# A new table of places: the steps of three overlapping batches merged into one order per engine

## The chip, the core and the metric

The kernel runs on one core of a Trainium2 chip. A core has five engines that each work through their own instructions in order: PE (TensorE, the matrix unit; its weight loads are listed apart as PEld), DVE (VectorE), ACT (ScalarE), POOL (GpSimd) and SP (SyncE, which here only starts transfers). They meet through semaphores. The metric is the device time of one execution in microseconds (us); lower is better.

## The reference

Two decoder layers over `x` of 32 batches, 128 tokens and 128 features, six sublayers in all, each with a residual and a layer norm:

```python
x = _layernorm(x + _L0_attn_ref(x, w_qkv, w_proj))                 # Nystrom attention, 16 heads, 64 landmarks
x = _layernorm(x + _L0_xattn_ref(x, ctx_1024, ...))                # cross attention, 16 heads of 8, relative bias
x = _layernorm(x + _L0_ffn_ref(x, Wr, br, W1, b1, W2, b2))         # 8 experts, the best one per token
x = _layernorm(x + _L1_attn_ref(x, Wq, Wk, Wv, Wo, bo))            # causal attention, 16 heads of 8
x = _layernorm(x + _L1_xattn_ref(x, ctx, ctx, mask, ...))          # masked cross attention, 16 heads of 64
x = _layernorm(x + _L1_ffn_ref(x, fc1_A, fc1_B, ...))              # h = gelu(x @ W1); h @ W2
# inside the Nystrom attention, per head, six times:
KV = K @ V;  V = 0.25 * V @ (13 * I - KV @ (15 * I - KV @ (7 * I - KV)))
```

All numbers are float32. The batches do not depend on one another.

## The kernel before, in words

A prologue loads all weights and composes the two matrices of the last feed-forward. Then the 32 batches run, each in two parts. The first part, `nystrom`, is the first sublayer; it has one set of buffers (stream 2) and one batch is in it at a time. The second part, `rest`, is the other five sublayers; it has two sets of buffers (lanes 0 and 1), and even and odd batches alternate. So three batches are in work at once: one in `nystrom`, two in `rest` at different depths.

Each engine's program is written as Python generators, one for `nystrom` and one for `rest`, which yield a name after each step. A step is a small group of instructions with the waits ahead of it. Names that begin with `n.` belong to `nystrom`; `r1.` is the first cross attention, `rm.` the experts, `r2.` the causal attention, `ry.` the masked cross attention, `rf.` the last feed-forward, and `r.ln1` to `r.ln4` the layer norms between them. The same name on two engines is the part of a stage that each engine does. The names that the prediction uses:

- On PE, `n.proj` is the projection of a new batch, `n.a0` to `n.a3` and `n.b0`, `n.b1` the score products, `n.e3T0`, `n.e3T1`, `n.e1T0`, `n.e1T1` transposes of exponentials, `n.col0`, `n.col1` column sums, `n.kk0`, `n.kk1` and `n.y0` the start values of the iteration, `n.ln` the transpose of the finished first layer norm. `n.Skg` and `n.Wkg` are the two products of round k (0 to 5) of the iteration for half g of the heads. Between `n.Skg` and `n.Wkg` ACT copies PSUM out (L984) and DVE makes two passes (L1265, L1267); between `n.Wkg` and the next `n.S` ACT scales (L990) and DVE adds (L1275).
- On PE, `rm.h0` to `rm.h3` and `rm.y0` to `rm.y3` are the first and second products of the experts, `rm.drop` adds the gate's exclusion to the first two (L789, L811). ACT makes the hidden values of `rm.h0` and `rm.h2` (L1052), DVE those of `rm.h1` and `rm.h3` (L1411).
- `r.lnN` on PE transposes the normalised rows; it waits for DVE L1186, which waits for POOL L1100 (a power), which waits for three statistics on DVE (L1173 to L1175) after the residual (L1180). ACT then copies the transposed block (L942).
- `ry.tN` on PE turns a group of probabilities, `ry.s23` makes scores, `ry.out` is the output product (L911). `rf.h` and `rf.out` are the two products of the last feed-forward.
- On SP, `rf.ln` stores the result (L503), `r1.ctxT` loads the context of the batch after next of the same lane (L494), and `r1.ctx` its rows and mask.

What sets the order of the work is a table, `PLACES`. For each engine it gives each step a place in microseconds from the start of its batch. The function `run` adds `number * PERIOD` for each batch, sorts all steps of all batches by that, and lets the generators run in that order. The places set the order only; when a step runs is decided by the semaphores and by what stands ahead of it on its engine.

PSUM is what ties steps of one stream together: a stream of `nystrom` has two banks and a lane has three. A step that writes a bank waits until the engine that read it is done. `n.e3T0` for instance waits for the exponentials of `n.b0` (L965), since it writes over their scores.

## Time and profile before

| | us |
|---|---|
| median of 3 runs | 2956.56 |
| lowest and highest | 2953.51, 2956.67 |
| the profiled execution | 2956.45 |
| its span in the trace | 2954.7 |

| engine | busy us | share of the span |
|---|---|---|
| PE | 2632.2 | 89% |
| DVE | 2101.3 | 71% |
| ACT | 1337.7 | 45% |
| POOL | 568.6 | 19% |

The page of the profile divides the span in 40 slices of 74 us. PE is at nine tenths or more in all but four at the start and two or three at the end. Busy counts pipelined matmuls as they overlap, so a full PE is 100% and not more.
### The profile page before, as it was taken

To read this page: it belongs to the slowest core of one execution; us is meant where nothing else is said; L and a number is where in the kernel's file an instruction comes from. 1 tells how busy PE (TensorE), PEld (TensorE's weight loads), DVE (VectorE), ACT (ScalarE), POOL (GpSimd) and SP (SyncE) were. 2 spreads that over 40 slices of the span, in tenths; PEclk is the share of its full clock that TensorE was granted. 3 is DMA by queue.
4 is the path that set the end of the run, shared out by engine and by line. 5 is a ranking of instruction groups with operands and counts; after the bars stand their busy time and mean duration, and the time that the engine had idled before them with its cause. 6 is when DMAs were issued, how large, how long until landed. Compare 5 with 4: busy or idle time off the path is not lost.

```text
span 2954.7 us, 79744 instructions
## 1 busy us (share of the span) xinstructions
PE 2632.2 (89%) x32768; PEld 2140.1 (72%) x32768; DVE 2101.3 (71%) x6528; ACT 1337.7 (45%) x4773; POOL 568.6 (19%) x644
## 2 busy tenths in 40 slices
PE   6789999999999999999999999999999899999975
PEld 4677777777777777777777777777777777777753
DVE  3367777777777777777777777777777777777763
ACT  1234444544444454444444444445454444444432
POOL 0012112221211222112122211122211122221121
PEclk8699999999999999999999999999999999999996
DMA  5000000000000000000000000000000000000000
GB/s 233 6 6 4 7 5 7 7 7 7 4 7 6 7 7 7 7 4 7 5 7 7 7 4 7 6 6 7 7 4 7 6 6 7 7 7 3 5 5 2
DMA packets 29465, 34.71 MB, mean 12 GB/s; under 512 B 3240, under 2 KB 27824, under 8 KB 28464
## 3 DMA queue, kind: packets, MB, share of 16 engines
q1 hardware_dynamic: 29104, 29.62, 2.9%
q8 instruction: 261, 4.28, 0.6%
q14 instruction: 100, 0.82, 0.1%
HBM read 27.51 MB, written 2.10 MB: 10 GB/s over the span
## 4 chain that ended last, share of the span: by engine, by line
PE 75%; DVE 14%; ACT 6%; issue 3%; POOL 0%; POOLq 0%; DVEq 0%; ACTq 0%
PE ps L516 40%; PE ps L519 13%; PE ps L798 5%; PE ps L781 4%; PE ps L703 4%; PE ps L865 2%; PE ps L911 2%; DVE wz L1267 2%; DVE small L1310 2%; DVE small L1234 1%; PE ps L789 1%; ACT ey L990 1%; PE ps L925 1%; PE ps L702 1%; ACT probs L1015 1%
## 5 line engine op out<-in xcount | busy, mean ns | idle before, releaser
L1100 POOL TENSOR_TENSOR small<-small,weights 128x1 f32<-128x1 f32 x256 | 141.4, 552 | 1269.1 <-DVE small L1175 1269.1
L984 ACT COPY ss<-ps 128x288 f32<-128x288 f32 x384 | 152.7, 414 | 425.4 <-PE ps L516 419.4
L1317 DVE COPY probsT<-ps 128x512 f32<-128x512 f32 x384 | 264.3, 688 | 93.9 <-PE ps L519 93.6
L1310 DVE TENSOR_REDUCE small<-ps 128x4 f32<-128x512 f32 x384 | 263.3, 686 | 86.5 <-PE ps L703 48.7
L516 PE MATMUL ps<-ey 64*64 64x72 f32 x6144 | 267.4, 228 | 63.5 <-DVE ey L1275 62.9
L516 PEld LDWEIGHTS ps<-ey 64*64 64x64 f32 x6144 | 221.4, 133 | 126.7 <-ACT ey L990 74.5
L1015 ACT ACTIVATE probs<-ps,small 128x128 f32<-128x128 f32 x1024 | 294.3, 382 | 4.9 <-DVE small L1311 4.9
L1111 POOL TENSOR_SCALAR k_alone_q_o<-qk_v,weights 128x512 f32<-128x512 f32 x128 | 224.0, 1756 | 233.2 <-DVE qk_v L1328 195.7
L1117 POOL TENSOR_TENSOR probs<-probs,small 128x256 f32<-128x256 f32 x128 | 108.9, 851 | 802.5 <-DVE small L1450 802.5
L516 PE MATMUL ps<-wz,ss 64*64 64x72 f32 x6144 | 238.4, 222 | 17.3 <-DVE wz L1267 17.2
L519 PE MATMUL ps<-weights,probs 128*128 128x128 f32 x1536 | 244.9, 282 | 7.6 <-POOL probs L1117 7.3
L516 PEld LDWEIGHTS ps<-wz,ss 64*64 64x64 f32 x6144 | 206.6, 133 | 53.6 <-DVE wz L1267 32.2
L990 ACT ACTIVATE ey<-ps 128x288 f32<-128x288 f32 x320 | 133.2, 416 | 235.9 <-PE ps L516 227.4
L519 PEld LDWEIGHTS ps<-weights,probs 128*128 128x128 f32 x1536 | 173.5, 142 | 56.2 <-issue 34.6
L1067 ACT ACTIVATE probs<-ps,small 128x128 f32<-128x128 f32 x512 | 182.0, 408 | 15.2 <-DVE small L1311 15.2
L798 PE MATMUL ps<-weights,probs 128*128 128x128 f32 x1024 | 150.1, 292 | 36.9 <-ACT probs L1052 36.9
L1267 DVE SCALAR_TENSOR_TENSOR wz<-ey,ss 128x288 f32<-128x288 f32 (+1 forms) x384 | 167.5, 436 | 13.2
L798 PEld LDWEIGHTS ps<-weights,probs 128*128 128x128 f32 x1024 | 132.6, 200 | 45.6 <-ACT probs L1052 43.0
L954 ACT ACTIVATE e<-ps,small 128x128 f32<-128x128 f32 x256 | 80.4, 366 | 184.7 <-DVE small L1226 184.7
L1265 DVE TENSOR_TENSOR ss<-ss,ey 128x32 f32<-128x32 f32 x384 | 80.0, 208 | 103.2 <-ACT ss L984 103.2
L781 PE MATMUL ps<-x_T,weights 128*128 128x128 f32 x1024 | 151.5, 296 | 0.0
L703 PE MATMUL ps<-k_alone_q_o,qk_v 128*128 128x512 f32 x256 | 148.3, 664 | 0.0
(199 smaller groups left out, 5617.5 us busy)
## 6 DMA issues: line engine op xcount, KB each, us to landing
weights<-in_wpack SPq DMA_DIRECT2D x1, 5703.5 KB
fc_B<-in_b SPq DMA_DIRECT2D x2, 2048.0 KB, 13.9
fc_A<-in_a SPq DMA_DIRECT2D x2, 2048.0 KB, 23.9
x_in_rows<-in_x SPq DMA_DIRECT2D x32, 64.0 KB, 1.8
x_in_T<-in_xT SPq DMA_DIRECT2D x32, 64.0 KB, 1.8
ctx_T<-in_ctxT SPq DMA_DIRECT2D x32, 64.0 KB, 2.0
ctx_rows<-in_ctx SPq DMA_DIRECT2D x32, 64.0 KB, 2.0
mask_i<-in_mask SPq DMA_DIRECT2D x32, 64.0 KB, 2.0
```

The costliest lines, as they stand in the source:

```text
L516: return mmul(dst, lhsT, rhs, start=True, stop=True)
L519: return nc.tensor.transpose(dst, src, ident)
L703: mm = mmul(to, qc(s), k_alone(s, g), start=False, stop=True, skip_group_check=True)
L781: mmul(bank(s, t % 2, 128 * c, 128), w("m_1", 512 * t + 128 * c, 128), xTs[s][:], start=(c == 0), stop=False, skip_group_check=True)
L798: mm = mmul(bank(s, 2, 256, D), hidden_T(s, t)[:, 2 * (e % 2) + c], w("m_2", (2 * e + c) * 128, 128), start=False, stop=(e == EXPERTS - 1 ...
L990: nc.scalar.mul(ey[:, ps], src, 0.25).then_inc(sem("newton_act", s), 1)
L1015: ins = nc.scalar.activation(probs(s, g)[:, j], bank(s, SCORE_BANK[g], 128 * j, 128), ACT.Exp, bias=sm(s, "nb", 4 * g + j, 1), scale=SC8)
L1067: ins = nc.scalar.activation(probs(s, g)[:, j], bank(s, g % 2, 128 * j, 128), ACT.Exp, bias=sm(s, "nb", 4 * g + j, 1), scale=SC64, accum_o ...
L1111: nc.gpsimd.tensor_scalar(k_alone(s, g), k4(s), w("gmask", g, 1), None, ALU.mult).then_inc(sem("a_k23", s), 1)
L1267: V.scalar_tensor_tensor(wz[:, ps, a:PW], ey[:, ps, a:PW], 3.0, ss[:, ps, a:PW], ALU.mult, ALU.add).then_inc(sem("newton_dve", s), 1)
L1310: link(V.tensor_reduce(sm(s, "mx", 4 * g, 4), bank(s, b).rearrange("p (a b) -> p a b", a=4), AX, ALU.max))
L1317: V.tensor_copy(probsT(s, n % 4).rearrange("p a b -> p (a b)"), bank(s, 2)).then_inc(sem("pT", s), 1)
```

## The change

The instructions are the same; the table of places is new for PE, ACT, POOL and DVE, with a new `PERIOD`, and `run` now lets a place be lower than that of the step ahead of it in its stream. Such a step takes the place of the step ahead, so that it stands right behind it. Steps of one stream keep their order; what moves is how the steps of the three streams stand among one another. SP's order comes out as before.

```diff
-PERIOD = 79.71
+PERIOD = 79.85700
 PLACES = {
...
     "pe": (
-        "n.proj 0.09  n.v 4.15  n.a0 4.91  n.a1 6.58  n.a2 7.01  n.a3 10.04  n.b0 14.27  n.b1 15.28  "
...
+        "n.proj -12.541  n.v -2.469  n.a0 -0.413  n.a1 4.916  n.a2 7.927  n.a3 10.019  n.b0 13.655  n.b1 15.252  "
...
     def run(engine, nystrom, rest):
 
         n_steps, r_steps = (steps(text) for text in PLACES[engine])
-        order = sorted((number * PERIOD + place, lane, number, k, name)
-                       for number in range(BATCHES) for lane, work in ((NYS, n_steps), (number % LANES, r_steps))
-                       for k, (name, place) in enumerate(work))
+        order = []
+        for lane in (0, 1, NYS):
+            last = -1e9
+            for number in range(BATCHES):
+                if lane in (NYS, number % LANES):
+                    for k, (name, place) in enumerate(n_steps if lane == NYS else r_steps):
+                        last = max(last, number * PERIOD + place)
+                        order.append((last, lane, number, k, name))
+        order.sort()
```

The diff adds 11 lines above the code, so L516 of before is L527 in the changed kernel, L519 is L530, and so on. In the rows of order below, `ps2` and names that end in `_2` belong to `nystrom`, `ps0` and `ps1` to the two lanes.

**Place 1.** PE in the middle of the program, where a new batch enters `nystrom` and the experts' second products begin (`x_first` is `n.ln`, L789 and L811 `rm.drop`, `x_in_T` `n.proj`, L798 `rm.y0`, L859 and L865 `ry.s23`). Before:

```order
L859 MATMUL ps0<-mask_add0,ident_bf 128x512 x2
L865 MATMUL ps0<-k8_0,k_alone_q8_o8_0 128x128 x8
L519 MATMUL ps2<-weights,x_first0 128x128
L789 MATMUL ps1<-not_gateT1,dropped 128x256 x4
L811 MATMUL ps1<-expert_b2,gateT1 128x128
L516 MATMUL ps2<-x_in_T_2,weights 128x128 x2
L798 MATMUL ps1<-weights,probs1 128x128 x4
```

The same place in the changed kernel:

```order
L800 MATMUL ps1<-not_gateT1,dropped 128x256 x4
L822 MATMUL ps1<-expert_b2,gateT1 128x128
L870 MATMUL ps0<-mask_add0,ident_bf 128x512 x2
L876 MATMUL ps0<-k8_0,k_alone_q8_o8_0 128x128 x8
L530 MATMUL ps2<-weights,x_first0 128x128
L527 MATMUL ps2<-x_in_T_2,weights 128x128 x2
L809 MATMUL ps1<-weights,probs1 128x128 x4
```

`rm.drop` stands ahead of `ry.s23` and `n.ln` now, and nothing is left between `n.ln` and `n.proj`.

**Place 2.** PE some 15 us of work later, from `n.b0` to the causal attention's first scores (`k_landmarks` is `n.b0` and `n.b1`, `x_rows1` `r.ln2`, `x_rows0` `r.ln4`, `ffn_w1` `rf.h`, `x_T1` `r2.proj`, `e3_2` `n.e3T0` and `n.e3T1`). Before:

```order
L516 MATMUL ps2<-k_landmarks_2,q1_2 128x256 x2
L519 MATMUL ps1<-weights,x_rows1 128x128
L516 MATMUL ps2<-k_landmarks_2,q1_2 128x256 x2
L516 MATMUL ps1<-x_T1,weights 128x128 x2
L516 MATMUL ps1<-weights,x_T1 128x128
L519 MATMUL ps0<-weights,x_rows0 128x128
L516 MATMUL ps0<-x_T0,ffn_w1 128x128 x4
L702 MATMUL ps1<-causal_bf,ident_bf 128x512
L703 MATMUL ps1<-k_alone_q8_o8_1,qk_v8_1 128x512
L519 MATMUL ps2<-weights,e3_2 128x128 x8
```

The same place in the changed kernel (L809 is `rm.y2` and `rm.y3`):

```order
L527 MATMUL ps2<-k_landmarks_2,q1_2 128x256 x2
L809 MATMUL ps1<-weights,probs1 128x128 x4
L527 MATMUL ps2<-k_landmarks_2,q1_2 128x256 x2
L809 MATMUL ps1<-weights,probs1 128x128 x4
L530 MATMUL ps0<-weights,x_rows0 128x128
L530 MATMUL ps2<-weights,e3_2 128x128 x4
L527 MATMUL ps0<-x_T0,ffn_w1 128x128 x4
L530 MATMUL ps1<-weights,x_rows1 128x128
L530 MATMUL ps2<-weights,e3_2 128x128 x4
L527 MATMUL ps1<-x_T1,weights 128x128 x2
```

`rm.y2` and `rm.y3` stand between and behind the two `n.b` steps, `r.ln4` is ahead of `r.ln2`, and `n.e3T0` comes right behind `r.ln4`, before `rf.h`.

ACT in the same stretch (L965 of before is `n.b0` and `n.b1`, L942 the copies of the `r.ln` steps, L1007 `r2.q`, L1084 and L1085 `rf.h`, L971 `n.e3T0` and `n.e3T1`). Before:

```order
L942 COPY x_T1<-ps1 128x128
L965 ACTIVATE e1_2<-ps2,small2 128x64 x8
L1007 COPY qk_v8_1<-ps1 128x128
L942 COPY x_T0<-ps0 128x128
L965 ACTIVATE e1_2<-ps2,small2 128x64 x8
L1084 ACTIVATE probs0<-ps0 128x512
L1085 COPY probs0<-ps0 128x512
L971 COPY e3T_2<-ps2 128x512 x2
```

The same place in the changed kernel:

```order
L976 ACTIVATE e1_2<-ps2,small2 128x64 x8
L953 COPY x_T0<-ps0 128x128
L976 ACTIVATE e1_2<-ps2,small2 128x64 x8
L953 COPY x_T1<-ps1 128x128
L982 COPY e3T_2<-ps2 128x512 x2
L1018 COPY qk_v8_1<-ps1 128x128
L1095 ACTIVATE probs0<-ps0 128x512
L1096 COPY probs0<-ps0 128x512
```

The second group of exponentials stands ahead of the copy for `r2.proj`, and the two copies of `n.e3T` ahead of `r2.q` and `rf.h`.

**Place 3.** PE in round 3 of the iteration (`ey_2` x16 or two x8 is a pair of `n.S` steps, `wz_2,ss_2` a pair of `n.W` steps, `x_norm0` `ry.xT`, L516 with `k_alone_q8_o8_1` `r1.s3`, `probs1` a turn of `r1`). Before:

```order
L516 MATMUL ps2<-ey_2 64x72 x8
L516 MATMUL ps1<-k_alone_q8_o8_1,qk_v8_1 128x128 x4
L519 MATMUL ps1<-weights,probs1 128x128 x4
L516 MATMUL ps2<-wz_2,ss_2 64x72 x16
L516 MATMUL ps2<-ey_2 64x72 x8
L519 MATMUL ps0<-weights,x_norm0 128x128
```

The same place in the changed kernel:

```order
L527 MATMUL ps2<-ey_2 64x72 x16
L530 MATMUL ps0<-weights,x_rows0 128x128
L527 MATMUL ps1<-probsT1,v9_1 32x128 x4
L527 MATMUL ps2<-wz_2,ss_2 64x72 x16
L530 MATMUL ps0<-weights,x_norm0 128x128
L527 MATMUL ps1<-k_alone_q8_o8_1,qk_v8_1 128x128 x4
L527 MATMUL ps2<-ey_2 64x72 x16
```

Before, `n.S40` stands right behind the pair `n.W30`, `n.W31`; now `ry.xT` and `r1.s3` are between them.

## Rows read from the trace of the kernel before

**Rows 1.** Stretch table: us, busy of PE, PEld, DVE, ACT, POOL, PE clock, DMA.

```profile
500.00:2500.00 2000.00, 1831.17 (x23414) 1496.90 (x23415) 1494.51 (x4663) 956.33 (x3423) 405.82 (x459) 0.98 0.02 6
```

**Rows 2.** Waits of PE from 500 to 2500 us: total, times, longest.

```profile
PE ps L516 <- DVE ey L1275: 46.2, 69, 1.1
PE ps L519 <- DVE x_rows L1186: 41.7, 46, 1.3
PE ps L798 <- ACT probs L1052: 27.1, 23, 1.2
PE ps L516 <- ACT x_T L942: 16.3, 46, 0.4
PE ps L519 <- ACT oT L993: 14.1, 20, 0.7
PE ps L516 <- DVE wz L1267: 8.6, 23, 0.4
PE ps L516 <- issue: 7.3, 7, 1.5
```

**Rows 3.** Timeline of PE: start, us, what, idle before; `n.b0`, `r.ln4`, scores, transposes.

```profile
1508.60 1.02 PE L703 MATMUL ps<-k_alone_q_o,qk_v 128*128 128x512 f32 x2
...
1512.25 1.10 PE L519 MATMUL ps<-weights,e 128*128 128x128 f32 x8
...
1587.06 1.03 PE L516 MATMUL ps<-k_landmarks,q 128*128 128x256 f32 x4
...
1591.06 0.33 PE L519 MATMUL ps<-weights,x_rows 128*128 128x128 f32 x1 [1.33 <-DVE x_rows L1186]
...
1593.20 1.92 PE L703 MATMUL ps<-k_alone_q_o,qk_v 128*128 128x512 f32 x2
1594.91 1.62 PE L519 MATMUL ps<-weights,e 128*128 128x128 f32 x8
```

**Rows 4.** Stretch table after the wait for `r.ln4`, columns as in rows 1.

```profile
1594.00:1596.00 2.00, 2.00 (x8) 1.32 (x7) 0.96 (x4) 0.31 (x1) 0.00 (x0) 0.50 0.00 0
```

**Rows 5.** Timeline of PE around `rm.y0`.

```profile
1570.85 0.60 PE L789 MATMUL ps<-not_gateT,dropped 8*128 8x256 bf16 x4
...
1573.49 1.16 PE L798 MATMUL ps<-weights,probs 128*128 128x128 f32 x8 [1.18 <-ACT probs L1052]
```

**Rows 6.** Timeline of ACT around the same place, and at `n.b0`.

```profile
1571.00 0.27 ACT L942 COPY x_firstT<-ps 128x128 f32<-128x128 f32 x1 [1.58 <-PE ps L519]
...
1572.29 1.15 ACT L1052 ACTIVATE probs<-ps,weights 128x128 f32<-128x128 f32 x4
...
1589.05 1.75 ACT L965 ACTIVATE e<-ps,small 128x64 f32<-128x64 f32 x8 [0.56 <-DVE small L1235]
```

**Rows 7.** Timeline of PE in rounds 3 and 4 of the iteration.

```profile
1544.13 1.22 PE L516 MATMUL ps<-wz,ss 64*64 64x72 f32 x32
1546.41 0.72 PE L516 MATMUL ps<-ey 64*64 64x72 f32 x16 [1.06 <-DVE ey L1275]
```

**Rows 8.** Timeline of DVE at `n.b0`, `ry.out`, and `r2.k0` with `r2.k1`.

```profile
1588.12 0.69 DVE L1234 TENSOR_REDUCE small<-ps 128x8 f32<-128x512 f32 x1
...
1588.93 0.29 DVE L1180 TENSOR_TENSOR res<-ps,x_plus_bo 128x128 f32<-128x128 f32 x1
...
1589.80 0.15 DVE L1175 TENSOR_SCALAR small<-small 128x1 f32<-128x1 f32 x1
...
1591.64 1.31 DVE L1337 TENSOR_SCALAR k_alone_q_o<-qk_v,weights 128x512 f32<-128x512 f32 x2
```

**Rows 9.** Timeline of PE: `rf.out` and the next `r1.proj`.

```profile
1511.20 1.16 PE L925 MATMUL ps<-ffn_w,probs 128*128 128x128 f32 x8 [0.28 <-DVE probs L1488]
...
1519.27 1.13 PE L516 MATMUL ps<-x_firstT,weights 128*128 128x128 f32 x8 [1.52 <-issue]
```

**Rows 10.** Timeline of SP between the two.

```profile
1515.24 0.43 SPq L494 DMA_DIRECT2D ctx_T<-in_ctxT  x1
```

**Rows 11.** The view of line 494, all 32 loads.

```profile
DMA to landing us min/median/max: 1.8/2.0/3.9
```

More of the change, by code:

```diff
@@ L64 @@
 BATCHES = B
-PERIOD = 79.71
+PERIOD = 79.85700
 PLACES = {
     "sp": (
-        "n.xT 2.07  n.x 75.75  ",
-        "r1.ctxT 108.30  r1.ctx 108.36  rf.ln 267.37  ",
+        "n.xT 2.075  n.x 75.755  ",
+        "r1.ctxT 108.300  r1.ctx 108.360  rf.ln 267.370  ",
     ),
     "pe": (
[15 rows of a table removed]
[18 rows of a table added]
     ),
     "act": (
[10 rows of a table removed]
[11 rows of a table added]
     ),
     "pool": (
-        "n.lm0 2.76  n.lm1 4.47  n.out 79.01  ",
-        "r1.k2 110.76  r1.k3 110.76  r1.ctx 128.37  r1.out 143.88  rm.out 173.96  r2.xbo 178.38  r2.k2 182.76  "
-        "r2.k3 185.43  r2.out 201.37  ry.stats 203.06  ry.xbo 206.33  ry.p0 217.41  ry.p1 224.91  ry.p2 238.73  "
-        "ry.p3 251.28  ry.out 262.23  rf.out 262.65  ",
[4 rows of a table added]
     ),
     "dve": (
[16 rows of a table removed]
[17 rows of a table added]
     ),
```

89 rows, old and new, of the table PLACES are left out of this document.

## The prediction

> **What bounds the kernel now.** I read four views in this order: the page, the stretch table, the list of waits, the timelines of one batch. The stretch table shows a steady state. From 500 to 2500 us PE is busy for 1831 of 2000 us, DVE for 1495, ACT for 956 [rows 1]. Waits that come once a batch are listed 23 times there [rows 2], so a batch takes 2000 / 23 = 87.0 us, of which PE works 79.6 us and stands idle (2000 - 1831) / 23 = 7.3 us. PE is the bound, and the change leaves its instructions as they are. What an order can win is the 7.3 us of idle time and what the clock loses through it.
>
> The list of waits says where the 7.3 us are [rows 2]; the totals divided by 23 are, per batch: 2.0 us until DVE has finished a `n.W` step for the next `n.S` (three places), 1.8 us for normalised rows (`r.ln3`, `r.ln4`), 1.2 us for the experts' hidden values at `rm.y0`, 0.7 us for a transposed block (`rm.gate`, `rf.h`), 0.6 us at `n.rows`, 0.4 us at an `n.W`, 0.3 us under "issue" at `r1.proj`. They recur at the same steps in every batch, so each is a round trip through another engine with too little PE work laid over it.
>
> The clock is the second loss. It is 0.98 over the steady state [rows 1]. After the 1.33 us wait of `r.ln4` it falls to 0.50, the level of 1.2 GHz [rows 3, 4]. There a pair of score products takes 1.92 us where the same takes 1.02 at full clock, and eight transposes 1.62 where they take 1.10 [rows 3]: 1.4 us lost, and I take 1.5 with the matmul next to them. With 0.98 as the mean, 4% of 87 us is at the low level and half of that, 1.7 us a batch, is lost, a little over one fall a batch.
>
> **The change, waits that go.** Here I lay the new order over the durations of the old trace. A round trip is hidden when the PE work between its two PE steps is at least as long as the trip.
>
> `n.S40` (place 3): `n.W30` and `n.W31` take 1.2 us and `n.S40` comes 1.06 us behind them [rows 7]. The trip is 1.6 to 2.3 us, since DVE has other copies ahead of its addition. Now `ry.xT` and `r1.s3`, some 1.2 us, stand between, so the cover grows from 0.6 to 1.8 us, and DVE has fewer steps ahead. The same holds at `n.S21` and `n.S50`, which have the transposes and `r1.v3` before them. I cost the 2.0 us at nothing, and the 0.4 us at `n.W00` as well, where `r2.t1` has come between.
>
> `rm.y0` (place 1): ACT needs 1.15 us for the hidden values after `rm.drop`, and it came to them only at 1572.29, since the copy of `x_first` and that of `n.q` stood ahead [rows 5, 6]. Now `rm.drop` is followed by `ry.s23` (sixteen matmul records and two mask products, by the eight records of rows 5 some 1.6 us), `n.ln` and `n.proj` (0.9 us together) before `rm.y0`. 2.5 us against a trip of 1.3 us: the 1.2 us go.
>
> `r.ln4` (place 2): behind `ry.out` stand now `n.b0`, `rm.y2`, `n.b1`, `rm.y3`, 0.9 + 1.0 + 0.9 + 1.0 = 3.8 us (a group's 1.03 overlaps its neighbour by 0.1 [rows 3], and 1.16 by 0.15 [rows 5]). The trip is the residual and statistics on DVE, 1588.93 to 1589.95, 1.0 us [rows 8], then 1.1 us through POOL and the rows until PE starts at 1591.06 [rows 3], and up to 1.3 us of queue on DVE (the reduction, its scaling, and what runs before them): 3.4 us. The wait goes, and with it that of `rf.h`, which follows it. `r.ln3` has the pairs `n.W2`, `n.S3` and the step `r1.s2` as new cover, over 3 us against 0.5 that it lacked. `n.rows` and `rm.gate` each have one more step ahead (`ry.t0` and `r.ln1`; `n.rows`).
>
> Together 46.2 + 41.7 + 27.1 + 16.3 + 14.1 + 8.6 = 154.0 us over 23 batches, 6.7 us a batch [rows 2].
>
> **Waits that come.** Five I can price.
>
> 1. `n.proj`, place 1: it writes the bank from which ACT copies `x_first`. `rm.drop` covered that copy before. Now nothing does: 0.27 us [rows 6] and about 0.1 us on either side, 0.4 us.
> 2. `n.e3T0`, place 2: it writes over the scores of `n.b0`. From the end of `n.b0` on PE, DVE has 0.2 us left of what it does, then `ry.out` 1.0 us, the reduction with its scaling 0.9 us [rows 8], and ACT 1.75 us [rows 6]: 3.85 us. PE has `rm.y2`, `n.b1`, `rm.y3` and `r.ln4`: 3.0 us. Wait 0.9 us. If the DVE queue is empty it is nothing; if it is longer by the tail of `rm.h3` it is 1.9 us.
> 3. `n.e3T1` needs the next 1.75 us group on ACT and has `rf.h` and `r.ln2` as cover: 0.35 us. Behind it ACT has two copies and `r2.q` in line, for which `n.col0` and `r2.s0` wait: 0.45 us.
> 4. `n.e1T0` needs `n.rd` on DVE. Since `r2.k0` and `r2.k1` (1.31 us [rows 8]), `r2.v`, `rf.h` and `r2.m0` are ahead of it, and PE has one step fewer between: 0.7 us, from 0 to 1.5 us.
> 5. `r1.proj`: it needs the context that SP loads once `rf.out` of the batch before in its lane has gone through DVE, POOL, DVE and the store. Before, PE worked from 1512.36, the end of `rf.out`, to 1517.75, and the load was issued at 1515.24 with 2.0 us to land: ready at 1517.24, 0.5 us to spare [rows 9 to 11]. In 7 of 23 batches it landed late and PE waited 7.3 / 7 = 1.04 us [rows 2], that is 1.5 us late. Now half of `n.e1T` is before `rf.out` and `r2.t1` behind `r1.proj`: 1.45 us of cover less, and the chain shortens by 0.45 us, as `r2.t0` comes earlier on DVE and some wait falls in between. So 0.5 us in a usual batch, 2.0 in a late one, 0.96 on average, 0.6 us more than before.
>
> Four round trips that lack 0.1 to 0.15 us each (`ry.t2`, `n.S11`, `n.kk1`, `n.S31`) make 0.5 us. Some fifteen others come out with less than 0.2 us to spare; I add 0.4 us for them. The sum is 0.4 + 0.9 + 0.8 + 0.7 + 0.6 + 0.5 + 0.4 = 4.3 us. Its ends: with every estimate at its low end 2 us, with the DVE queue longer at items 2 to 4, 7 us.
>
> **The clock.** The 1.33 us wait after which it fell goes. New is a stretch with items 2 to 4 close together, 2.4 us idle in 10 us of work with many transposes. I expect one fall there in most batches, so 0.7 of the 1.7 us come back. The ends are 1.7 us won (no fall) and 1.3 us lost (two).
>
> The Trainium skill, page "TensorE: Matmul & The Clock Gate", section "A second HAM failure mode: psum-queue depth-cycling", says that short idle times between groups of matmuls, if they are frequent enough, make the clock swing between its levels. This speaks against an order that trades a few long waits for many short ones; the trace agrees in part, as a wait of 1.33 us was enough for a fall.
>
> **The sum.** Per batch: -6.7 + 4.3 - 0.7 = -3.1 us. Batches 0 and 1 fill the pipeline and the last is alone at the end, where there is nothing to interleave and the order changes nothing, so I count 30 batches: -93 us. The profiled execution took 2956.45 us, the median is 2956.56, so both give 2864 us.
>
> **The rivals.**
>
> A. The new waits are shorter, and the clock stays up. The durations with which I laid out the order are slightly long, since neighbours overlap. Then 2.1 us of new waits and 1.7 us from the clock: -6.7 + 2.1 - 1.7 = -6.3 us, 30 times is -189, 2767 us. For it speaks that each new wait is under 1 us; against it that four of them come one after another.
>
> B. The waits go as forecast, but the clock falls twice a batch, in the `n.e3T` stretch and at place 1, where `rm.drop`, `ry.s23` and the new wait of `n.proj` follow one another. Two falls cost 3.0 us against 1.7: -6.7 + 4.3 + 1.3 = -1.1 us, -33, 2923 us. This is the skill's rule at full force.
>
> C. The waits only move: DVE is the true pace maker. Its 65 us of work a batch leave 22 us of gaps, but in the order it may queue behind PE events so that each saving comes back elsewhere: 0 a batch, 2957 us. Against it: PE is busy 92% in the steady state, DVE 75%.
>
> D. Slower. The place is the stretch from `n.b0` to `n.e1T0`. ACT has both 1.75 us groups ahead of the copies for `r2.proj` and `n.e3T` (place 2), and each group waits for a reduction on DVE that stands behind `n.a3`, `n.p0` and `ry.out`. If these queues come late by both groups, PE waits 3.5 us more there, and the clock falls twice: -1.1 + 3.5 = +2.4 us, +71, 3027 us. It decides once the waits in this stretch are over 4.5 us with two falls, against the 2.4 us that I found.
>
> E. The table does not do what it says: excluded, since places 1 to 3 stand as described.
>
> **How the numbers follow.** Forecast 50%, its own range 2820 to 2905 (new waits of 3 to 5.7 us); A 18%, B 14%, C 7%, D 11%. A change of 0.2%, 6 us, is what a measurement can tell from none. Faster: forecast, A, B and a little of C, 83%. Same: 5%, out of C. Slower: D and a part of C, 12%. The range for 8 in 10 goes from 2780, which leaves out half of A, to 2945, which leaves out D and most of C.
>
> **What would show it.** PE idle in the steady state of about 5 us a batch and a batch of 84 us. No wait of `rm.y0`, `r.ln4` and `n.S` over 0.3 us; new waits of L530 with `e` for ACT L976, 0.9 us, of L527 with `x_in_T` for ACT L953, 0.4 us, and of L527 with `x_firstT` in nearly every batch. The clock at 0.98 or 0.99. Waits of the `n.S` steps that stay, or more than 4.5 us of idle time from `n.b0` to `n.e1T0`, would make it wrong; a clock under 0.97 would be B.

## The result, and the profile after

| us | before | after |
|---|---|---|
| median | 2956.61 (4 runs, 2953.51 to 2961.44) | 2755.98 (4 runs, 2754.63 to 2758.38) |
| the profiled execution | 2956.45 | 2757.24 |
| its span | 2954.7 | 2755.4 |

The ratio is 0.932, with a 95% interval of 0.931 to 0.934: 201 us faster. The forecast was 2864 us with a range that ended at 2780, so the sign was right, and the size was less than half of what came. The time is that of rival A (2767 us), to which the forecast gave 18%.

The row of the clock on the page of after, in 40 slices as before, and the stretch table of after, 500 to 2500 us, with the columns of [rows 1]:

```profile
PEclk9899999999999999999999999999999999999996
```

```profile
500.00:2500.00 2000.00, 1920.21 (x25316) 1576.36 (x25314) 1632.39 (x5036) 1031.16 (x3695) 458.15 (x495) 1.00 0.03 7
```

PE is idle for 80 us of the 2000, where it was for 169 [rows 1], and the clock is 1.00. The waits of PE in the same stretch, as the view lists them:

```profile
PE ps L527 <- DVE k_landmarks L1216: 13.7, 24, 0.6
PE ps L527 <- issue: 13.4, 25, 1.8
PE ps L527 <- ACT x_firstT L953: 12.0, 24, 0.5
PE ps L530 <- ACT e L976: 11.8, 25, 0.5
PE ps L530 <- DVE small L1254: 10.5, 25, 0.4
PE ps L527 <- DVE ey L1286: 4.8, 26, 0.2
PE ps L713 <- DVE k_alone_q_o L1348: 2.3, 15, 0.2
```

The waits of 46.2, 41.7, 27.1 and 16.3 us that headed [rows 2] are gone, down to 4.8 us of `ey`. Of the five that stand first now, four are priced in the forecast (`n.proj`, `n.e3T0`, `n.e1T0`, `r1.proj`), and the first is not: `n.a0`, which waits for the landmarks that DVE makes.

To compare kernels I use a sum per batch, read from PE's timeline between the starts of `r1.proj` from 600 to 2400 us (20 to 22 batches). Idle is the sum of the waits. The clock's loss is half of the time that PE was busy at the lower level. The rest, by this estimate, is what PE's work would take at the upper level.

| us per batch | period | idle | lost to the clock | the rest |
|---|---|---|---|---|
| before | 87.07 | 7.39 | 2.03 | 77.64 |
| after | 80.67 | 3.27 | 0.08 | 77.33 |
| difference | -6.40 | -4.12 | -1.95 | -0.31 |

Between the first and the last `r1.proj` of the program lie 31 periods: 2680.4 us before and 2482.6 after, -197.7 us, that is -6.4 each. The stretch ahead of the first `r1.proj` is 5.2 us shorter, and the one behind the last is 3.7 us longer. So nearly all of the gain is in the periods.

Place 1 in the timeline of PE after (start, us, what, idle before):

```profile
1376.86 0.59 PE L870 MATMUL ps<-mask_add,ident_bf 128*128 128x512 bf16 x2
1377.38 1.16 PE L876 MATMUL ps<-k,k_alone_q_o 64*128 64x128 f32 x16
1378.47 0.33 PE L530 MATMUL ps<-weights,x_first 128*128 128x128 f32 x1
1379.30 0.68 PE L527 MATMUL ps<-x_in_T,weights 128*128 128x128 f32 x4 [0.50 <-ACT x_firstT L953]
1379.82 1.06 PE L809 MATMUL ps<-weights,probs 128*128 128x128 f32 x8
...
1382.89 0.92 PE L527 MATMUL ps<-k,q_landmarks 128*128 128x192 f32 x4 [0.57 <-DVE k_landmarks L1216]
```

The expert product (L809) starts without a wait, where it had 1.18 us [rows 5]. `n.proj` waits 0.50 us, as item 1 said (0.4). Then comes the wait of 0.57 us that nothing in the forecast named.

Place 2, from `n.b0` to `n.e3T1`, PE:

```profile
1392.29 1.03 PE L527 MATMUL ps<-k_landmarks,q 128*128 128x256 f32 x4
1393.15 1.05 PE L809 MATMUL ps<-weights,probs 128*128 128x128 f32 x8
1394.04 1.03 PE L527 MATMUL ps<-k_landmarks,q 128*128 128x256 f32 x4
1394.91 1.05 PE L809 MATMUL ps<-weights,probs 128*128 128x128 f32 x8
1395.80 0.27 PE L530 MATMUL ps<-weights,x_rows 128*128 128x128 f32 x1
1396.54 0.66 PE L530 MATMUL ps<-weights,e 128*128 128x128 f32 x4 [0.47 <-ACT e L976]
...
1398.34 0.66 PE L530 MATMUL ps<-weights,e 128*128 128x128 f32 x4
```

Its counterparts on DVE and on ACT:

```profile
1393.75 0.15 DVE L1186 TENSOR_SCALAR small<-small 128x1 f32<-128x1 f32 x1
1393.82 0.68 DVE L1245 TENSOR_REDUCE small<-ps 128x8 f32<-128x512 f32 x1
1394.54 0.17 DVE L1246 TENSOR_SCALAR small<-small 128x8 f32<-128x8 f32 x1
```

```profile
1394.74 1.74 ACT L976 ACTIVATE e<-ps,small 128x64 f32<-128x64 f32 x8 [1.80 <-DVE small L1246]
...
1396.47 1.82 ACT L976 ACTIVATE e<-ps,small 128x64 f32<-128x64 f32 x8
```

`r.ln4` (1395.80) has no wait any more. `n.b0` ends at 1393.32, and DVE begins its reduction 0.50 us later; the forecast had put 1.2 us there (0.2 of what DVE is doing and 1.0 of `ry.out`). `ry.out` was nearly done by then. In the kernel before, DVE came to `n.b0` later: in the 8 us ahead it waited 0.65 and 0.99 us for PE, and it had the residual and the statistics of `r.ln2` to do (L1416, L1173 to L1175, 1584.82 to 1585.90). After, DVE has no idle time there, and these statistics come later. So the wait of `n.e3T0` is 0.47 us and not 0.9. `n.e3T1` starts at 1398.34, 0.05 us after the second group of exponentials ends (1396.47 + 1.82), and does not wait at all.

### The profile page after: what moved, and what is told of

Same layout as the page of the kernel before. It is cut to its first block, busy times and chain, and to the rows that moved or that the text cites. A ratio compares the mean times of both kernels' runs of the same rounds, so it can differ in the third digit from the quotient of the medians.

```text
span 2755.4 us, 79744 instructions
## 1 busy us (share of the span) xinstructions
PE 2552.7 (93%) x32768; PEld 2080.8 (76%) x32768; DVE 2122.9 (77%) x6528; ACT 1334.1 (48%) x4773; POOL 594.1 (22%) x644
## 4 chain that ended last, share of the span: by engine, by line
PE 70%; DVE 21%; issue 3%; ACT 2%; POOL 2%; POOLq 0%; DVEq 0%
PE ps L527 41%; PE ps L530 13%; PE ps L792 3%; DVE small L1321 3%; PE ps L876 3%; PE ps L922 2%; PE ps L714 2%; PE ps L809 2%; DVE k_alone_q_o L1348 1%; DVE qk_v L1315 1%; PE ps L870 1%; PE ps L936 1%; DVE small L1184 1%; DVE k L1214 1%; POOL probs L1128 1%
## 5 line engine op out<-in xcount | busy, mean ns | idle before, releaser
L1122 POOL TENSOR_SCALAR k_alone_q_o<-qk_v,weights 128x512 f32<-128x512 f32 x128 | 233.2, 1832 | 265.7 <-DVE qk_v L1339 209.9
L530 PE MATMUL ps<-weights,probs 128*128 128x128 f32 x1536 | 250.8, 285 | 14.8 <-POOL probs L1128 11.4
L527 PE MATMUL ps<-wz,ss 64*64 64x72 f32 x6144 | 246.2, 224 | 7.3 <-DVE wz L1278 5.0
L527 PE MATMUL ps<-ey 64*64 64x72 f32 x6144 | 242.8, 227 | 7.5 <-DVE ey L1286 6.9
L527 PEld LDWEIGHTS ps<-wz,ss 64*64 64x64 f32 x6144 | 211.0, 133 | 46.6 <-DVE wz L1278 22.0
L527 PEld LDWEIGHTS ps<-ey 64*64 64x64 f32 x6144 | 211.6, 133 | 42.4 <-issue 32.5
L530 PEld LDWEIGHTS ps<-weights,probs 128*128 128x128 f32 x1536 | 166.3, 141 | 84.0 <-ACT probs L1026 27.2
L1278 DVE SCALAR_TENSOR_TENSOR wz<-ey,ss 128x288 f32<-128x288 f32 (+1 forms) x384 | 158.8, 413 | 13.2
L965 ACT ACTIVATE e<-ps,small 128x128 f32<-128x128 f32 x256 | 80.0, 364 | 172.6 <-DVE small L1237 172.6
L527 PEld LDWEIGHTS ps<-k_alone_q_o,qk_v 128*128 128x128 f32 x1024 | 128.8, 194 | 15.6 <-issue 15.3
L976 ACT ACTIVATE e<-ps,small 128x64 f32<-128x64 f32 x512 | 113.2, 367 | 55.0 <-DVE small L1246 55.0
L792 PE MATMUL ps<-x_T,weights 128*128 128x128 f32 x1024 | 139.7, 280 | 0.0
L527 PE MATMUL ps<-k_alone_q_o,qk_v 128*128 128x128 f32 x1024 | 136.1, 276 | 0.3 <-ACT oT L1032 0.3
L809 PE MATMUL ps<-weights,probs 128*128 128x128 f32 x1024 | 135.9, 276 | 0.0
```

The source lines that it names most:

```text
L527: return mmul(dst, lhsT, rhs, start=True, stop=True)
L530: return nc.tensor.transpose(dst, src, ident)
L792: mmul(bank(s, t % 2, 128 * c, 128), w("m_1", 512 * t + 128 * c, 128), xTs[s][:], start=(c == 0), stop=False, skip_group_check=True)
L809: mm = mmul(bank(s, 2, 256, D), hidden_T(s, t)[:, 2 * (e % 2) + c], w("m_2", (2 * e + c) * 128, 128), start=False, stop=(e == EXPERTS - 1 ...
L1122: nc.gpsimd.tensor_scalar(k_alone(s, g), k4(s), w("gmask", g, 1), None, ALU.mult).then_inc(sem("a_k23", s), 1)
L1278: V.scalar_tensor_tensor(wz[:, ps, a:PW], ey[:, ps, a:PW], 3.0, ss[:, ps, a:PW], ALU.mult, ALU.add).then_inc(sem("newton_dve", s), 1)
```

## The experiments

**Where the gain is.** Seven kernels hold both tables. They build both orders, cut each engine's order at three points where the same steps are done in both, and take each piece from one or the other. The pieces of a batch are: the iteration (`r2.t0` to `n.W50`, place 3), the middle (`n.W50` to `rm.y0`, with place 1), and the late piece (`rm.y0` to `r2.t0`, with place 2). `TAKE` names the order outside of batches 4 to 29, then that of the three pieces; `spliced` puts the order together from them.

```diff
+CUTS = {
+    "pe": (("r2.t0", "r2.t0"), ("n.W50", "n.W50"), ("rm.y0", "rm.y0")),
...
...
-        order.sort()
+        order = spliced(engine)
```

`iter_new`:

```diff
+TAKE = ('old', 'new', 'old', 'old')
```

> The old order everywhere, but for batches 4 to 29 the new order in one third of the round: from r2.t0 to n.W50, the iteration. Theory (each stretch wins its own waits, and the clock falls belong to the waits of rm.y0 and r.ln4): the three n.S waits, r.ln3 and n.W00 go, 2.0 + 0.5 + 0.4 us, some 0.4 us comes: -2.5 us a batch, 26 times is -65 us against before, about 2892 us; the clock keeps its 1.2 falls a batch. Rival (the order wins as a whole: a stretch alone only passes its savings on to the next old wait): less than -25 us. Rival (the clock comes back with any shorter wait): falls go down too, below -90 us.

`mid_new`:

```diff
+TAKE = ('old', 'old', 'new', 'old')
```

> The old order everywhere, but for batches 4 to 29 the new order in the second third: from n.W50 to rm.y0 (place 1). Theory: the waits of n.rows, rm.gate and rm.y0 go (0.7 + 0.35 + 1.18), n.proj waits 0.5 us, -1.75 us a batch, and with rm.y0 goes the half of the clock falls that follows it, 13 in 23 batches at 1.5 us, -0.85: -2.6 us a batch, 26 times is -68 us, about 2889 us. Rival (order as a whole): less than -25 us. Rival (the falls come from the matmuls of few rows in rm.drop and ry.s23, not from the wait): the falls at rm.y0 stay, -45 us.

`late_new`:

```diff
+TAKE = ('old', 'old', 'old', 'new')
```

> The old order everywhere, but for batches 4 to 29 the new order in the last third: from rm.y0 to r2.t0 (place 2). Theory: the waits of r.ln4 and rf.h go (1.33 + 0.35), those of n.a0, n.e3T0 and n.e1T0 come (0.55 + 0.47 + 0.42), -0.25 us a batch, and the falls after r.ln4, 15 in 23 batches, go, -1.0: -1.25 us a batch, 26 times is -32 us, about 2924 us. Rival (order as a whole): -10 us or slower. Forecast on record (this stretch keeps a fall and 2.4 us of new waits): +1 us a batch, +25 us.

`inside_new`:

```diff
+TAKE = ('old', 'new', 'new', 'new')
```

> The new order in all three thirds for batches 4 to 29, the old one for the filling and the emptying of the pipeline. Theory: the steady state's whole gain, 26 times -6.4 us = -166 us, about 2790 us, and the sum of the three single thirds, -165 us. Rival (order as a whole): far more than the sum of the three. Rival (a good part of the gain is in filling and emptying): above 2800 us.

The three that undo one piece each, `iter_old`, `mid_old` and `late_old`:

```diff
+TAKE = ('new', 'old', 'new', 'new')     # iter_old
+TAKE = ('new', 'new', 'old', 'new')     # mid_old
+TAKE = ('new', 'new', 'new', 'old')     # late_old
```

> The new order, but for batches 4 to 29 the old one in the iteration (from r2.t0 to n.W50). From the first four runs: this third gave -82.6 us where all else was old, -3.26 us a batch. If the thirds add up, the loss is +82 us on the changed kernel's 2756, about 2838 us, and three waits of n.S for DVE of 2.0 us a batch come back. On the clock: theory (falls belong to long waits, whatever the stretch): the waits that come back are 1.06 us at most and in the old order had no falls behind them, so 0 to 2 falls in 20 batches. Rival (any idle time adds to a fall): 5 or more falls in 20 batches.

> The new order, but for batches 4 to 29 the old one from n.W50 to rm.y0. If the thirds add up: +57 us, 2813 us. The waits of rm.y0 (1.18), n.rows and rm.gate come back. On the clock: theory (the 1.18 us wait of rm.y0 makes the clock fall in half of the batches): 8 to 12 falls in 20 batches, at rm.y0. Rival (a fall needs more than its wait: with the late third new, rm.y0 kept its wait and had 1 fall in 20): 0 to 3 falls, and the time is then about 2800.

> The new order, but for batches 4 to 29 the old one from rm.y0 to r2.t0. If the thirds add up: +37 us, 2793 us. The waits of r.ln4 (1.33) and rf.h come back, those of n.e3T0 and n.e1T0 go. On the clock: theory: 12 or more falls in 20 batches, all after r.ln4. Rival: 0 to 3 falls, and the time about 2770.

Measured, with the sum per batch from each trace and the clock's falls by its record in the trace:

| kernel | median us | ratio (95%) | period | idle | clock | rest | falls in batches |
|---|---|---|---|---|---|---|---|
| before | 2956.61 | | 87.07 | 7.39 | 2.03 | 77.64 | 24 in 20 |
| iter_new | 2863.84 | 0.972 (0.968 to 0.977) | 83.81 | 4.97 | 2.04 | 76.81 | 24 in 20 |
| mid_new | 2889.87 | 0.980 (0.976 to 0.985) | 84.69 | 6.35 | 0.94 | 77.40 | 11 in 20 |
| late_new | 2909.47 | 0.987 (0.982 to 0.992) | 85.62 | 6.63 | 0.76 | 78.23 | 9 in 20 |
| inside_new | 2782.15 | 0.944 (0.940 to 0.949) | 80.60 | 3.17 | 0.08 | 77.34 | 1 in 22 |
| iter_old | 2843.63 | 0.963 (0.959 to 0.966) | 83.91 | 5.62 | 0.08 | 78.21 | 1 in 21 |
| mid_old | 2789.11 | 0.945 (0.941 to 0.948) | 82.07 | 4.19 | 0.48 | 77.40 | 6 in 21 |
| late_old | 2789.59 | 0.944 (0.940 to 0.948) | 81.91 | 4.16 | 1.21 | 76.54 | 15 in 21 |
| after | 2755.98 | 0.932 (0.931 to 0.934) | 80.67 | 3.27 | 0.08 | 77.33 | 1 in 22 |

The steady state alone brings 164 us (26 batches of 6.4 us are 166), and the rest of the 201 comes from the batches around them, give or take the 10 us between the two medians of before (2946.48 and 2956.61). In 28 timings beside these experiments the kernel before took 2930.95 to 2967.50 us, and its granted clock went from 0.968 in the fastest to 0.952 in the slowest: its spread goes with its clock. Half of the steady state's gain is the iteration: 82.6 us alone (the median of before in that comparison was 2946.48), and 88 us lost when it alone is undone (2843.63 against 2755.98, from two comparisons). The other two pieces bring 57 and 37 us alone, and each costs about 33 us when it alone is undone.

The pieces do not quite add up: 176 us one by one, 164 together, 155 by what is lost when each is undone. The clock is the main reason why the single gains are too large: of the 2.03 us a batch that it loses in before, the new middle alone takes 1.09 away and the new late piece alone 1.27. Against what was expected, `mid_new`, `iter_old` and `late_old` came within 6 us. `iter_new` came 28 us lower: its idle time fell by 2.42 us a batch, as expected (2.5), and 0.83 us came off the "rest". `late_new` came 15 us lower, since eight of the nine falls at `rm.y0` went, though its wait stayed. `mid_old` came 24 us lower, with three falls at `rm.y0` where 8 to 12 were expected; its rival named 0 to 3 falls and 2800 us.

The waits of PE in `iter_new`, 500 to 2500 us, show what it took away and what it left:

```profile
PE ps L634 <- DVE x_rows L1301: 32.0, 24, 1.3
PE ps L913 <- ACT probs L1167: 28.2, 24, 1.2
PE ps L631 <- ACT x_T L1057: 17.1, 48, 0.4
...
PE ps L631 <- DVE ey L1390: 4.1, 23, 0.2
```

The wait for `ey` went from 46.2 us [rows 2] to 4.1, and half of the `x_rows` waits (`r.ln3`, 46 down to 24 of them). Those of `rm.y0` and `r.ln4` are as before, and so are the clock's 24 falls in 20 batches. In `iter_old`, the opposite, 48.2 us of `ey` come back and the clock has one fall:

```profile
PE ps L631 <- DVE ey L1390: 48.2, 72, 1.1
```

So the three waits of the iteration, 0.7 us on average and 1.1 at most, take no clock away, while `rm.y0` and `r.ln4` do.

The "rest" moved too, which the forecast had no term for. It goes by the piece: against the 77.33 us of after it is 0.9 us higher with the old iteration (78.21), 0.8 lower with the old late piece (76.54), and the same with the old middle (77.40). PE's records are longer next to a wait: the `n.S` products take 7.72 us a batch in before and 7.15 in after, with three waits less, but the `n.W` products take 6.96 and 7.18. A cost of starting again after each wait does not account for it. After has 11.1 waits of over 0.05 us a batch; `ctx_early` and `all_three` below have 2 fewer and the same rest (77.31 and 77.34), `lm0_late` 2.4 fewer and 77.16. What makes the rest is open. From before to after it is 0.31 us of 6.40.

**The waits that came.** Four kernels each take away one of the new waits, or more, from the changed kernel. `ctx_early` has SP issue the load of the next context rows once PE has read the last ones, ahead of the store of the result:

```diff
-        "r1.ctxT 108.300  r1.ctx 108.360  rf.ln 267.370  ",
+        "r1.ctxT 108.300  r1.ctx 108.360  r1.next 125.000  rf.ln 267.370  ",
...
-            if s.turn:
-                sp.wait_ge(sem("proj", s), last_use("proj", s, 3))
-            sp.dma_start(cTs[s][:], ctxT[s.number]).then_inc(sem("ctxT_in", s), 16)
+            if not s.turn:
+                sp.dma_start(cTs[s][:], ctxT[s.number]).then_inc(sem("ctxT_in", s), 16)
...
+            if s.number + LANES < BATCHES:
+                sp.wait_ge(sem("proj", s), at("proj", s, 3))
+                sp.dma_start(cTs[s][:], ctxT[s.number + LANES]).then_inc(sem("ctxT_in", s), 16)
+            yield "r1.next"
```

> The changed kernel, but SP loads the context of the batch after next right after r1.proj has read the last one, so that it no longer stands behind the store. Theory (r1.proj waits for this load, 0.56 us a batch, and each wait costs 0.1 us more when PE starts again): -0.65 us a batch, 30 times is -20 us, 2736 us, and no wait of r1.proj of over 0.1 us. Rival (r1.proj waits for the statistics of rf.out or for the clearing of a bank, the load lands in time): 2756 us, and the wait stays. Rival (the time is passed on to n.S00 and n.W00, whose round trip loses its cover): -5 us.

Measured: 2730.60 us, ratio 0.925 (0.921 to 0.929), 25 us under after. The wait under "issue" is gone from the list, and the idle time is 2.70 us a batch against 3.27. The wait of `r1.proj` was for that load, as item 5 said. The period is 0.66 us shorter: 0.57 us of idle time and the one clock fall (0.08). The 0.1 us for starting PE again that the expectation adds does not show (rest 77.31 against 77.33).

`lm0_late` moves POOL's first pass of the landmarks behind `ry.p2`:

```diff
-        "n.lm0 -11.459  n.lm1 7.429  n.out 76.688  ",
+        "n.lm0 -1.050  n.lm1 7.429  n.out 76.688  ",
```

> The changed kernel, but on POOL n.lm0 stands behind ry.p2, as in the kernel before. In the changed kernel DVE's 64-column addition of n.lm1 takes 1.07 us where it takes 0.22 before, and it begins while POOL's n.lm0 runs. Theory (DVE is held by POOL's instruction, and n.a0 waits 0.57 us for that): the addition takes 0.22 us again, n.a0 and ry.t2 wait no more, -0.67 and 0.1 for the new start of PE: -0.8 us a batch, 30 times is -24 us, 2732 us. Rival (POOL only moves the collision to the next DVE instruction, the expert's relu or a copy): 2745 to 2760 us. Rival (it is the wait for ACT's n.k): no change.

Measured: 2730.49 us, ratio 0.924 (0.921 to 0.928), again 25 us. The reason stands in two timelines. After, POOL and DVE:

```profile
1380.47 1.55 POOL L1133 TENSOR_TENSOR q_landmarks<-q_landmark,weights 128x512 f32<-128x512 f32 x1 [3.13 <-DVE q_landmark L1214]
```

```profile
1380.17 0.22 DVE L1214 TENSOR_TENSOR q_landmark<-q 128x64 f32<-128x64 f32 x1
1380.43 0.69 DVE L1216 TENSOR_TENSOR q_landmarks<-q_landmark,weights 128x512 f32<-128x512 f32 x1
1381.04 1.07 DVE L1214 TENSOR_TENSOR k<-k 128x64 f32<-128x64 f32 x1
1382.14 0.69 DVE L1216 TENSOR_TENSOR k_landmarks<-k,weights 128x512 f32<-128x512 f32 x1
```

Two additions of one line and one shape take 0.22 and 1.07 us. The second runs from 1381.04 to 1382.11 beside POOL's pass, which ends at 1382.02. That pass is itself 1.55 us long, and its first half microsecond lies beside the DVE pass of 1380.43. The view of line 1214 of `lm0_late` (ns, least, median and most) has the same addition short in every batch:

```profile
L1214 DVE TENSOR_TENSOR k<-k x25: 216/218/221, 574.2 to 2488.3; 128x64 f32<-128x64 f32 x25
```

and that of after long in every batch:

```profile
L1214 DVE TENSOR_TENSOR k<-k x24: 1067/1068/1070, 576.3 to 2431.4; 128x64 f32<-128x64 f32 x24
```

In `lm0_late` POOL's pass stands elsewhere and takes 1.04 us:

```profile
1374.80 1.04 POOL L1133 TENSOR_TENSOR q_landmarks<-q_landmark,weights 128x512 f32<-128x512 f32 x1
```

The wait of `n.a0`, 0.57 us, is gone, and the 0.10 us of `ry.t2` with it. It is the one that the forecast did not have: it came from POOL's order, which I had not laid over DVE's.

The Trainium skill, page "SBUF — State Buffer", section "SBUF: two separate sides", says that DVE and GpSimd share a pair of ports, that a DVE operation with two inputs in SBUF and a GpSimd operation lock it for a whole instruction, and that the other one waits in full. The rows fit this to 0.15 us: if POOL waits out the DVE pass (1380.43 to 1381.12) and then takes its own 1.04 us, it ends at 1382.16, and it ended at 1382.02; the addition ends 0.09 us behind that. This rule spoke against the change, and the forecast did not weigh it.

`proj_late` puts `rm.y0` between `n.ln` and `n.proj` on PE, and `lm0_proj` does both:

```diff
-        "n.proj -12.541  n.v -2.469  ...
+        "n.proj -2.940  n.v -2.469  ...
```

> The changed kernel, but on PE n.proj stands behind rm.y0, so that rm.y0 covers the copy of x_first. The wait of n.proj, 0.5 us, goes. Theory (a wait of a later step of the same stream, n.a0 on DVE's n.lm1, takes all of it, since the chain n.proj, n.q, n.lm, n.a0 starts 0.5 us later): n.a0 waits 1.0 us, 2750 to 2762 us. Rival (n.a0 waits for POOL and DVE's own queue, not for this chain): -0.6 us a batch, 2738 us.

> Both edits: n.lm0 behind ry.p2 on POOL and n.proj behind rm.y0 on PE. Theory: without POOL's collision the chain to n.a0 has room for 0.5 us: -0.67 - 0.5 and 0.2 for new starts, -1.3 us a batch, -39 us, 2717 us. Rival (the chain is as long as its cover): as lm0_late alone, 2732 us.

Measured: 2759.0 us, ratio 0.933 (0.930 to 0.937), and 2733.48 us, ratio 0.926 (0.921 to 0.930). The 0.50 us of `n.proj` go and bring nothing. The wait of `n.a0` in `proj_late` is 1.00 us where it was 0.57 (13.7 us in total before the move), and `n.v` now waits 0.13:

```profile
PE ps L527 <- DVE k_landmarks L1216: 24.9, 25, 1.0
```

With both, `n.a0` waits only 0.15 us, but `n.v` waits 0.13, and the rest is 77.37 us against 77.16 of `lm0_late`. So the second kernel came at the rival's 2732 us and not at the 2717 of the theory. `n.proj` feeds the chain to the landmarks; a later start hides its own wait and moves the chain behind it back.

`all_three` joins the three edits, `ctx_lm0` only the two that won:

> The two edits and the early load of the context, which alone gave 2731 against 2756 us. If the three add up: 2756 - 25 - 39 = 2692 us. If n.proj's wait only moves to n.a0: 2707 us.

> The new table with two of its new waits taken out together: the loads of the next context rows issued ahead of the rf.ln store (as ctx_early) and POOL's n.lm0 behind ry.p2 (as lm0_late). Theory (the two waits are separate terms of the batch): 2756 - 25 - 25 = 2706, ratio about 0.915, the waits of r1.proj and n.a0 both under 0.1 us a batch, and as fast as all_three (2710). Rival (all_three's proj move carried part of it): 2715 to 2725.

Measured: 2710.06 us, ratio 0.917 (0.914 to 0.920), and 2710.38 us, ratio 0.916 (0.914 to 0.917). The 2692 us of three separate terms did not come, since the move of `n.proj` adds nothing. The two others give 46 us under after, of 50 expected from their sum: they are separate terms. It beats both kernels. In `ctx_lm0` PE is idle 2.02 us a batch, and its three largest waits in 500 to 2500 us are:

```profile
PE ps L530 <- ACT x_firstT L956: 12.6, 25, 0.5
PE ps L533 <- ACT e L979: 12.3, 26, 0.5
PE ps L533 <- DVE small L1257: 10.9, 26, 0.4
```

**What makes the clock fall.** `mid_old` and `late_old` each keep one wait after which the clock fell before (`rm.y0`, 1.18 us, and `r.ln4`, 1.33 us). `mid_old` had 6 falls in 21 batches, of which three at `rm.y0`. `late_old` had 15: 12 at `r.ln4`, and three behind long waits of `r1.proj` (1.25 to 1.62 us). `late_new` keeps the wait at `rm.y0` in every batch and has only one fall there in 20 where before has 9. The length of the wait alone does not decide: `n.a0` waits 1.00 us in every batch of `proj_late` without a fall, and two waits of `r1.proj` in `lm0_proj`, 1.93 and 1.67 us, went without and with one.

Nor does a fall need a wait. Two of the nine falls of `late_new` stand behind waits of `r1.proj`, and six begin at one place where PE has not waited for 7 us. The rows of one of them, PE in `late_new`; the clock's record falls at 943.27:

```profile
936.32 0.72 PE L631 MATMUL ps<-ey 64*64 64x72 f32 x16 [0.33 <-DVE ey L1390]
...
940.09 1.10 PE L631 MATMUL ps<-wz,ss 64*64 64x8 f32 x32
...
941.28 1.07 PE L631 MATMUL ps<-ctx_normT,weights 128*128 128x128 f32 x8
942.28 1.10 PE L631 MATMUL ps<-ey,p 64*64 64x8 f32 x32
...
943.90 1.92 PE L631 MATMUL ps<-ctx_normT,weights 128*128 128x128 f32 x8
```

Ahead of the fall PE is busy without a gap, but with two groups of 32 products of 64 rows and 8 columns. Before and `iter_new` have one fall at this place, and `mid_old` has two, in three of these four without any idle time of PE in the 9 us ahead. All of these kernels hold the old middle piece; those with the new one have none there. No run takes these products apart from what stands around them.

Two more kernels add the earlier load of `ctx_early` to `mid_old` and `late_old`. It touches no wait of the old pieces and shortens the batch.

> mid_old (stretch n.W50 to rm.y0 in the old order, 6 clock falls in 21 batches) with the context load issued earlier, which takes about 0.65 us out of each batch and touches no wait of the old stretch. If a fall follows from the wait and what surrounds it: about 6 falls in 21 again, time 2789 - 25 = 2764. If it follows from how the wait stands in time: the count changes by more than 3, at 0.5 us a fall up to 5 us lower or 8 us higher.

> late_old (stretch rm.y0 to r2.t0 in the old order, 15 clock falls in 21 batches) with the context load issued earlier. If a fall follows from the wait and what surrounds it: about 15 falls in 21 again, time 2790 - 25 = 2765. If it follows from how the wait stands in time: the count changes by more than 3, time 2757 to 2768.

Measured: `mid_old_ctx` 2783.57 us, ratio 0.940 (0.938 to 0.942), 11 falls in 21 batches; `late_old_ctx` 2768.80 us, ratio 0.935 (0.934 to 0.937), 16 in 22. The forecast of unchanged counts, 2764 us, failed for the first; for the second 2765 was close. The load took 0.5 and 0.65 us of idle time out of the batch. In `mid_old_ctx` the five more falls took 0.41 us back, and 5.5 us are left of the 25; in `late_old_ctx` the clock's loss stayed as it was and 20.8 came through. Its count only looks the same: the three falls behind `r1.proj` went with their waits, and those at `r.ln4` rose from 12 in 21 to 16 in 22. PE's rows of `rm.y0` in `mid_old_ctx`, of six batches in a row:

```profile
577.74 1.85 PE L916 MATMUL ps<-weights,probs 128*128 128x128 f32 x8 [1.18 <-ACT probs L1170]
660.43 1.16 PE L916 MATMUL ps<-weights,probs 128*128 128x128 f32 x8 [1.18 <-ACT probs L1170]
741.50 1.78 PE L916 MATMUL ps<-weights,probs 128*128 128x128 f32 x8 [1.18 <-ACT probs L1170]
824.20 1.16 PE L916 MATMUL ps<-weights,probs 128*128 128x128 f32 x8 [1.18 <-ACT probs L1170]
905.27 1.71 PE L916 MATMUL ps<-weights,probs 128*128 128x128 f32 x8 [1.18 <-ACT probs L1170]
987.90 1.16 PE L916 MATMUL ps<-weights,probs 128*128 128x128 f32 x8 [1.18 <-ACT probs L1170]
```

and of three batches in a row of `mid_old`:

```profile
749.66 1.16 PE L913 MATMUL ps<-weights,probs 128*128 128x128 f32 x8 [1.18 <-ACT probs L1167]
831.03 1.16 PE L913 MATMUL ps<-weights,probs 128*128 128x128 f32 x8 [1.18 <-ACT probs L1167]
913.13 1.16 PE L913 MATMUL ps<-weights,probs 128*128 128x128 f32 x8 [1.18 <-ACT probs L1167]
```

The wait is 1.18 us in all nine rows. The eight matmuls behind it take 1.16 us at the upper level, and 1.7 to 1.85 in every second batch of `mid_old_ctx`, where the clock fell. A batch with a fall lasts 82.70 us there (741.50 to 824.20) and one without 81.07 (824.20 to 905.27): a fall costs 1.6 us, and not the 0.5 us of the expectation. But for one, the falls of that kernel come 163.8 us apart, two batches. One comes 81.9 us after the fall ahead of it, and from there on the falls stand in the batches of the other lane, so they do not belong to a lane. Taking out what the falls cost, the period is 81.6 us in `mid_old` and 81.0 in `mid_old_ctx`. I read this as follows: whether a wait of this length takes the clock down depends also on the moment at which it comes. The two kernels differ in the wait of `r1.proj` besides, some 50 us ahead, and no run moves the moment alone, so it is a reading and not shown. The Trainium skill, page "TensorE: Matmul & The Clock Gate", section "What's actually happening", says that the monitor behind the clock runs freely and does not start anew with the kernel. The counts do not speak against that; no run here shows the monitor itself.

The one fall of after between 500 and 2500 us, by the timeline of PE:

```profile
1492.35 1.69 PE L527 MATMUL ps<-x_firstT,weights 128*128 128x128 f32 x8 [1.80 <-issue]
```

It is the longest wait of that stretch, a load that landed late, and the eight matmuls take 1.69 us where the same take 1.13 elsewhere. The single falls of `inside_new`, `lm0_late` and `iter_old` follow such waits of `r1.proj` too, of 1.22, 1.11 and 1.37 us, while others as long brought none (1.38 us in after, 1.52 twice in before); `ctx_early`, `all_three` and `ctx_lm0`, which have no wait there, have no fall in 21 or 22 batches. The regular new waits, 0.6 us at most, brought none.

## Why the prediction was wrong

Per batch, in its own terms:

| step | forecast | measured |
|---|---|---|
| waits that go | -6.7 | -6.47: they were 6.73 in these batches, and 0.26 stay at `n.S` (0.19) and `n.W` (0.08) |
| 1. `n.proj` | +0.4 | +0.50 |
| 2. `n.e3T0` | +0.9 | +0.47 |
| 3. `n.e3T1`, `n.col0` with `r2.s0` | +0.8 | +0.29 |
| 4. `n.e1T0` | +0.7 | +0.42 |
| 5. `r1.proj` | +0.6 | +0.2 (0.56, from 0.36) |
| four small and the reserve | +0.9 | +0.16 (`ry.t2` 0.10, `r.ln2` 0.06) |
| `n.a0`, not forecast | 0 | +0.57 |
| the clock | -0.7 | -1.95 |
| PE's work itself | 0 | -0.31 |
| the wait of `rf.out` [rows 9], gone, not forecast | 0 | -0.28 |
| sum | -3.1 | -6.40 |

**Right.** PE's idle time was what could be won, and each named wait went: the terms of `n.S`, `rm.y0`, `r.ln3` and `r.ln4` are the three pieces of the splices. Items 1 to 5 were the right places, and the removal of items 1 and 5 by themselves shows their mechanisms. Rival B is out by the clock, C and D by the time: `late_new`, which holds D's place alone, is 37 us faster than before.

**Wrong, the sum of the new waits.** The step that says 4.3 us measured 2.61, and 2.04 without `n.a0`, which it did not have. Items 2 to 4 assumed that DVE comes to `n.b0` with its queue as it stood in before's trace; at place 2 it was 0.5 us and not 1.2. I had laid each new wait over the old timeline, and the old timeline holds waits of DVE for PE (0.65 and 0.99 us ahead of `n.b0`) and steps that the change moves away. The rows show this for `n.e3T0`; for items 3 and 4 I take the same cause, and no run tests it. The reserve of 0.4 us for fifteen steps "with less than 0.2 us to spare" and most of the 0.5 us for four more had next to no counterpart. What I did not see was a collision on engines that are not the bound (POOL with DVE), 0.57 us.

**Wrong, the clock.** The step "I expect one fall there in most batches" failed: 1 fall in 22. It took the new short waits, 2.4 us idle in 10 us, to act as one long one. As they came they are 1.2 us there, none over 0.47, and no fall follows; what 2.4 us would do, no run shows. `iter_old` has the new waits and the three of the iteration besides, 5.62 us idle a batch, and one fall in 21 batches. The forecast's loss before was also too small, 1.7 us where the record of the clock gives 2.03. The trace of before could have told it: 9 falls stood at `rm.y0`, 14 at `r.ln4`, and only one anywhere else, though `n.S` waited 60 times in those 20 batches. The rule of the Trainium skill that I weighed there (page "TensorE: Matmul & The Clock Gate", section "A second HAM failure mode: psum-queue depth-cycling"), that frequent short idle times make the clock swing, is not borne out by this order: after has 11.1 waits of over 0.05 us a batch, and the clock stays up.

**Wrong, the number of batches.** I counted 30; 31 periods were shortened, 6 us of the miss.

The two main terms lie in the same direction: new waits too long by 1.7 us and a clock gain too small by 1.25 us, together 2.9 of the 3.3 us that are missing per batch. Rival A named just that pair with 2.1 and 1.7 us. It came near, 11 us off in the time, partly by luck: its reason for shorter waits, overlapping neighbours, is not the one that the rows show, and it had neither `n.a0` (+0.57) nor `rf.out` (-0.28) and PE's work (-0.31), which cancel. Its chance of 18% was too low, since the clock's half of it stood in rows of before.

## What to carry to other kernels

Lay a new order over the old durations, but not over the old waits: queues behind a removed wait can be shorter too, and here the foreseen new waits came out at about half (2.0 of 4.3 us). Before giving the clock's loss a price, list after which waits it fell and after which it did not; here an order that shortened just those got the clock back whole. When one wait is hidden by moving a step later, look at the end of the chain that it starts (`n.proj`), and lay the engines that are not the bound over each other as well (POOL and DVE).

## What the runs showed of the hardware that was not expected

- A DVE addition of 128 x 64 took 1.07 us beside a POOL pass and 0.22 us without it, and the POOL pass 1.55 us against 1.04.
- The same wait of 1.18 us was followed by a fall of the clock in every second batch, in 9 of 20, in 3 of 21, or in one of 20, in kernels that differ only in the order or the period around it. A fall cost 1.6 to 1.7 us (two neighbouring batches of `mid_old_ctx`; half of PE's time at the lower level), more than the wait itself.
- The clock also fell in the middle of uninterrupted work: ten times at one place of the old middle piece, behind two groups of 32 products of 64 rows and 8 columns, with no wait of PE in the 6.9 us ahead.
- An order changed what the same matmuls take, beside their waits and the clock: 76.5 us a batch with the old late piece, 78.2 with the old iteration, 77.3 with neither.
